# A transformer layer on 8 cores: four PSUM banks in turn for the qkv projection, and one cast moved from VectorE to GpSimd

## The reference

```python
x = x + attn_a(layernorm(x))     # causal, rotary embedding, softmax
x = x + ffn(layernorm(x))
x = x + attn_b(layernorm(x))     # not causal, rotary, q and k normalised
x = x + ffn(layernorm(x))        # same weights as the first ffn

def ffn(x):
    h = bit_linear(x, w1)                      # 1024 -> 4096
    h = silu(depthwise_conv1d(h, conv_w))      # three taps along the tokens
    return bit_linear(h, w2)                   # 4096 -> 1024

def bit_linear(x, w):            # x rounded to integers by a scale per token,
    ...                          # w rounded to -1, 0, 1
```

## Time and profile before

| | us |
|---|---|
| median of the runs before (2 runs: 4828.32 and 4828.6) | 4828.46 |
| the profiled execution, its own time | 4822.62 |
| its span on the slowest core | 4821.1 |
| spans of the 8 cores | 4804.7 to 4821.1 |

### The profile page before, as it was taken

How to read it: one execution, slowest core, us unless ns; L and a number is a source line. 1 busy time by engine, 2 the same in 40 slices (tenths; PEclk the granted TensorE clock), 3 DMA queues, 4 the chain that set the end, 5 groups by cost and what they waited for, 6 DMA issues and landing times.

```text
span 4821.1 us, 43781 instructions; the slowest of 8 cores (4804.7 to 4821.1 us)
## 1 busy us (share of the span) xinstructions
PE 2901.5 (60%) x11610; PEld 993.1 (21%) x11610; DVE 1946.7 (40%) x3077; ACT 1947.7 (40%) x2092; POOL 506.5 (11%) x1034
## 2 busy tenths in 40 slices
PE   2455456656564456757545555777777835658665
PEld 0122111111112222323212221111111212223222
DVE  3323222222225676776533331010110166767763
ACT  0222145555440324224034444777777513242240
POOL 0000022222222001001001110000000110011010
PEclk9777666666676789989877777888878868889898
DMA  6333343322210123323231113000010001223224
GB/s 152 105 97 94 99 92 90 82 75 76 80 38 1 50 70 96 101 70 110 70 64 27 27 27 60 16 16 16 16 26 6 3 1 60 83 72 114 77 90 136
DMA packets 321185, 311.21 MB, mean 65 GB/s; under 512 B 213648, under 2 KB 226224, under 8 KB 320944
## 3 DMA queue, kind: packets, MB, share of 16 engines
q1 hardware_dynamic: 316272, 291.62, 21.4%
q0 software_dynamic: 4672, 16.79, 2.1%
HBM read 270.46 MB, written 50.46 MB: 67 GB/s over the span
## 4 chain that ended last, share of the span: by engine, by line
PE 29%; DVE 23%; ACT 18%; issue 12%; DMA 10%; POOL 4%; SPq 1%; DVEq 1%; ACTq 0%; POOLq 0%
PE pb L587 6%; PE pb L378 6%; PE pb L612 5%; ACT expqb L559 5%; PE squad L546 4%; DMA wq_tmp<-w2T 3%; ACT qkbfb L397 3%; PE squad L1065 3%; PE pb L659 2%; DMA wq_tmp<-w1T 2%; PE pb L908 2%; DVE hqi_B L1098 2%; DVE hqi_DD L1098 2%; DVE hdeq_DD L999 2%; DVE hdeq_B L999 2%
## 5 line engine op out<-in xcount | busy, mean ns | idle before, releaser
L559 ACT ACTIVATE expqb<-squad,kconst 128x1024 bf16<-128x1024 f32 x512 | 566.3, 1113 | 211.0 <-PE pb L587 167.2
L559 ACT ACTIVATE expqa<-squad,kconst 128x1024 bf16<-128x1024 f32 x320 | 351.2, 1112 | 304.8 <-PE pb L587 225.4
L587 PE MATMUL pb<-expqb,vbufb 128*65 128x512 bf16 x1024 | 363.4, 441 | 0.8 <-ACT expqb L559 0.8
L587 PE MATMUL pb<-expqa,vbufa 128*65 128x512 bf16 x640 | 258.8, 495 | 125.3 <-POOL expqa L571 117.5
L378 PE MATMUL pb<-Wqkva,lnTa 128*128 128x512 bf16 x768 | 212.0, 426 | 174.4 <-DVE lnTa L373 174.4
L1065 PE MATMUL squad<-xqfm_B,wbuf_B 128*128 128x512 bf16 x1024 | 246.5, 384 | 112.4 <-DVE hdeq_B L999 107.5
L1065 PE MATMUL squad<-xqfm_DD,wbuf_DD 128*128 128x512 bf16 x1024 | 246.2, 384 | 112.1 <-DVE hdeq_DD L999 109.3
L908 PE MATMUL pb<-w2buf_DD,hsilu_DD 128*128 128x512 bf16 x1024 | 265.7, 392 | 52.1 <-DMA w2buf_DD<-w2qT_d 30.5
L908 PE MATMUL pb<-w2buf_B,hsilu_B 128*128 128x512 bf16 x1024 | 263.2, 387 | 52.7 <-DMA w2buf_B<-w2qT_d 26.7
L546 PE MATMUL squad<-qbufb,kbufb 64*128 64x512 bf16 x1024 | 228.5, 436 | 108.6 <-ACT expqb L559 78.8
L1023 ACT ACTIVATE cvo_B<-hdeq_B,tapb_B,tapw_B 128x512 f32<-128x512 f32 x128 | 104.1, 813 | 433.6 <-POOL hdeq_B L1010 235.5
(11 more groups left out here) (219 smaller groups left out, 4284.4 us busy)
## 6 DMA issues: line engine op xcount, KB each, us to landing
wq_tmp<-w1T SPq DMA_DIRECT2D x64, 512.0 KB, 4.8
wq_tmp<-w2T SPq DMA_DIRECT2D x64, 512.0 KB, 4.0
wbuf_B<-w1qT_d SPq DMA_DIRECT2D x128, 256.0 KB, 2.6
w2buf_B<-w2qT_d SPq DMA_DIRECT2D x128, 256.0 KB, 2.7
wbuf_DD<-w1qT_d SPq DMA_DIRECT2D x128, 256.0 KB, 2.6
w2buf_DD<-w2qT_d SPq DMA_DIRECT2D x128, 256.0 KB, 2.8
x<-x SPq DMA_DIRECT2D x16, 512.0 KB, 28.7
w1qT_d<-wq_bf SPq DMA_DIRECT2D x32, 256.0 KB, 2.9
```

Of the source, the lines that this page charges most:

```text
L559: sb.op("act", lambda e, sqh=sqh, eb=eb: e.activation(out=expq[eb][:, 0:1024], in_=squad[:, sqh * 1024:(sqh + 1) * 1024], func=AF.Exp, sca ...
L587: sb.op("pe", lambda e, i=i, hi=hi, v0=v0, eb=eb, ob=ob, first=first, last=last: e.matmul(pbank[ob + hi][0:65, :], vbuf[i][:, v0:v0 + 65], ...
```

## The change

Two edits. In the first part of both attentions the six groups of a chunk take the banks `pbank[0]` to `pbank[3]` in turn instead of `pbank[0]` and `pbank[1]`; the keys follow. (The added `g=g` in three lambdas has no effect on what is issued.) In the quantising loop of the FFN the cast from int32 to bf16 is issued on POOL instead of DVE; its operands and keys are as before.

```diff
--- before.py
+++ after.py
@@ -373,36 +373,36 @@
         sb.op("dve", lambda e, i=i, tps=tps: e.tensor_copy(out=lnT[i][:], in_=tps),
               reads=[("sq", 0)], writes=[("lnT", i)])
         for g in range(6):
-            pb = pbank[g % 2]
+            pb = pbank[g % 4]
             for dc in range(NDC):
                 sb.op("pe", lambda e, i=i, dc=dc, g=g, pb=pb: e.matmul(
                     pb[:], lnT[i][:, dc * 128:(dc + 1) * 128],
                     Wqkv[dc][:, g * 512:(g + 1) * 512],
                     start=(dc == 0), stop=False),
-                    reads=[("lnT", i), ("Wqkv", dc)], writes=[("pb", g % 2)])
+                    reads=[("lnT", i), ("Wqkv", dc)], writes=[("pb", g % 4)])
             sb.op("pe", lambda e, g=g, pb=pb: e.matmul(
                 pb[:], onesbf[0:1, :], battrow[0:1, g * 512:(g + 1) * 512],
                 start=False, stop=True),
-                reads=[("onesbf",), ("battrow",)], writes=[("pb", g % 2)])
+                reads=[("onesbf",), ("battrow",)], writes=[("pb", g % 4)])
             if g < 4:
                 if causal:
                     dst = qkbf[i][:, g * 512:(g + 1) * 512]
-                    sb.op("act", lambda e, dst=dst, pb=pb: e.activation(
+                    sb.op("act", lambda e, dst=dst, pb=pb, g=g: e.activation(
                         out=dst, in_=pb[:], func=AF.Identity),
-                        reads=[("pb", g % 2)], writes=[("qkbf", i)])
+                        reads=[("pb", g % 4)], writes=[("qkbf", i)])
                 else:
                     dst = qkbf[i][:, g * 512:(g + 1) * 512].rearrange(
                         "p (h b a) -> p h a b", b=2, a=32)
                     src0 = pb[:].rearrange("p (h a b) -> p h a b", a=32, b=2)
-                    sb.op("act", lambda e, dst=dst, src0=src0: e.activation(
+                    sb.op("act", lambda e, dst=dst, src0=src0, g=g: e.activation(
                         out=dst, in_=src0, func=AF.Identity),
-                        reads=[("pb", g % 2)], writes=[("qkbf", i)])
+                        reads=[("pb", g % 4)], writes=[("qkbf", i)])
             else:
                 h0 = (g - 4) * 8
                 vv = vstage[i][:].rearrange("p (h c65) -> p h c65", c65=65)[:, h0:h0 + 8, 0:64]
-                sb.op("act", lambda e, pb=pb, vv=vv: e.activation(
+                sb.op("act", lambda e, pb=pb, vv=vv, g=g: e.activation(
                     out=vv, in_=pb[:].rearrange("p (h q) -> p h q", q=64), func=AF.Identity),
-                    reads=[("pb", g % 2)], writes=[("vstage", i)])
+                    reads=[("pb", g % 4)], writes=[("vstage", i)])
         if pending[0] is not None:
             pending[0]()
         qv = qkbf[i][:].rearrange("p (g2 h i2) -> p g2 h i2", h=2, i2=32)
@@ -1099,7 +1099,7 @@
                 out=hqi[:], in0=hsilu[:, jc * 512:(jc + 1) * 512], in1=squad[:, 0:512],
                 op=ALU.mult),
                 reads=[("hsilu", jc), ("sq", 0)], writes=[("hqi",)])
-            sb.op("dve", lambda e, jc=jc: e.tensor_copy(
+            sb.op("pool", lambda e, jc=jc: e.tensor_copy(
                 out=hqb_all[:, jc * 1024:jc * 1024 + 512], in_=hqi[:]),
                 reads=[("hqi",)], writes=[("hsilu", jc)])
             if jc == 0:
```

## The result

| | before | after |
|---|---|---|
| median of all runs, us | 4832.27 (10 runs) | 4888.02 (11 runs) |
| profiled execution: span of the slowest core | 4821.1 | 4871.7 |

The ratio of after to before is 1.0106, 95% interval 1.0079 to 1.0132: 51 us slower (38 to 64). The prediction was 118 us slower, with a range from 57 to 222 us (4885 to 5050 against 4828). The sign and the place are right; the size is less than half. The loss is clear of no change, but it lies within the 2% to which the prediction gave 34 in 100.

A forecast was written before the change was run, and what follows sets the result against it. No engine bounds the whole kernel; DVE's product and cast pace the quantising loop, ACT the second attention's first part. Banks 0, casts 109 and clock 9 make 118 us over 4828: 4946 us, range 4885 to 5050.

The forecast's parts named there:

- What bounds the loop: Quantising loop of the FFN: 32 DVE steps of 1.32 us, product and cast with gaps, plus a short end.
- The banks are worth nothing: First part of both attentions: four banks instead of two gain 0, bounds 0 and -24.3 us; ACT sets the pace.
- The step as product + handover + X + handover: Quantising loop, one block after the change: 0.686 + 0.21 + X + 0.10 = 0.996 + X us, against 1.32.
- X: Time of one quantising-loop cast on POOL, taken as 0.75 us; 256 casts add 109 us.
- the prediction's own sign: Quantising loop: the forecast is wrong if the cast L1102 on POOL takes under 0.67 or over 1.1 us.
- The handover from DVE to POOL at 0.21: Quantising loop: from the product's end on DVE to the cast's start on POOL, 0.21 us, read from L422.
- The clock, 9 us: Quantising loops' ends and next tiles' starts: a lower TensorE clock adds 9 us, bounds 0 and 17.
- Rival 1: Quantising loop: POOL casts as fast as it writes, 0.53 to 0.67 us; +53 to +88 us; 33 in 100.
- Rival 2: Quantising loop: integer conversion is slow on POOL, 1.1 us or more a cast; 5093 us at 1.29; 8 in 100.
- Rival 4: Quantising loop: DVE and POOL hinder each other, 0.33 us a cast, 84 us more, 5030; 1 in 100.
- The price from the skill: Quantising loop's cast on POOL: 769 ns for 512 elements from a skill page, adding 114 us instead of 109.
- Rival 3: Quantising loop: product and cast overlap, PE's 1.02 us sets the step, 77 us less, 4752; 2 in 100.

The follow-up runs named there:

- experiment 2: The kernel before with only the four banks, the cast staying on VectorE: ratio 0.9979 (0.9955 to 1.0002).
- experiment 7: The full change with hqi in f32, rounding to integers left out: the cast on GpSimd takes 0.609 us.
- experiment 13: The full change with the cast replaced by a GpSimd add of two different f32 tiles, hqi and amac, into bf16: the add takes 1.26 us.
- experiment 8: The full change with the cast replaced by a GpSimd add of hqi (f32) to itself: add 1.04 us, some 160 us slower than before.
- experiment 3: The full change with two hqi buffers and keys instead of one: ratio 0.9970 to the kernel before, 15 us faster than it.
- experiment 14: The full change with the cast on ScalarE instead of GpSimd, still one hqi buffer: ratio 1.0151 to the kernel before, 73 us slower.

## Why the prediction was right and wrong

- *What bounds the loop: right.* 32 steps of DVE set its length before; the round trip sets it after, with every product waiting for POOL's L1102 (105.1 us in 124 waits for the first FFN).
- *The banks are worth nothing: right*, as far as the times can tell (experiment 2) and by the stage's length in the traces, 467.3 and 465.4 us.
- *The step as product + handover + X + handover: right in form.* With the measured terms it gives 0.69 + 0.13 + 0.61 + 0.10 = 1.53, and 54 us for 256 blocks, against 51 measured.
- *X = 0.75: the term that was most out.* It measured 0.609, 0.141 less, or 36 us of the sum. By the prediction's own sign (L1102 under 0.67) the forecast was wrong. The text had the right figure, 0.62, from the copy of two columns and the memsets' 0.86 ns a column, and put it aside for two reasons. One was that the integer might cost something: experiment 7 shows that it doesn't. The other was half of the two-input row L669. That row adds two different tiles, and experiment 13 shows that such a second input costs 0.65 us where the first costs 0.43. The row to halve was L428 in the earlier trace rows, which squares one tile: (1.89 - 0.18) / 1024 / 2 is 0.83 ns a column, and with 0.18 that makes 0.61. The prediction's 1.63 ns a column mixed that row with L571, which reads two different tiles.
- *The handover from DVE to POOL at 0.21: out as well.* It measured 0.13, 0.08 less, or 20 us. I read it from one pair of rows and gave it no bounds, although shows another: L1010 starts 0.13 us behind the L999 that released it (started at 2001.97, 0.68 us long). The 0.21 holds a second semaphore wait, 0.06 us, that L1102 does not have behind VectorE's. The range was built from X alone, and that is why its lower end, +57 us, which needs X = 0.55 with 0.21, lies above the 51 us that came out with X at 0.609.
- *The clock, 9 us: about nothing.* The granted clock in the first loop is 0.95, as in the earlier trace rows, with PE busy 33.54 of 49.60 us (68%), not the 58% that the longer step would have made. The tile behind the third loop starts with eight matmuls in 1.89 us, the upper level, where the earlier trace rows had 3.32. And the earlier trace rows was not the rule: of the six tiles behind a quantising loop on the slowest core, four started in 1.89 us before the change and two at the lower level, and after it all six in 1.89. So the term was priced from an exception. In experiment 8, with a step of 1.97 us, the loop's granted clock is 0.85, so a longer step can lower it; 1.53 us did not.
- 36 + 20 + 9 = 65 of the 67 us by which the forecast missed: the mechanism was right, and three terms of its sum were too large.
- *Rival 1 (POOL casts as fast as it writes) is what happened* as to X: 0.609 lies in its 0.53 to 0.67, and the result in the band of no change that it named. Its 53 to 88 us carried the same 0.21; with 0.13 it reads 33 to 68.
- *Rival 2 (slow conversion) fell* with experiment 7. *Rival 4 (the engines hinder each other) fell* with experiment 3: 0.609 us for the cast, alone or beside the product. The product reads one operand from SBUF and one from PSUM. The Trainium skill, page "SBUF — State Buffer", section "SBUF: two separate sides", has the lock only for DVE instructions with two SBUF inputs or in a two-port mode. The trace of experiment 3 agrees: the loop was spared with overlap too.
- *The price from the skill*, 769 ns for 512 elements (the Trainium skill, page "GPSIMD Engine Reference", section "3.1 Elementwise — side-by-side cycle accounting"), was no better than mine. The same section has a second rate, 1.03 cycles an element for small loop bodies (its k ≤ 2). At the 1.2 GHz that it uses this is 0.86 ns, an estimate, and the measured 0.83 ns a column is near it. The prediction had cited the other of the two.
- *Rival 3's price was wrong.* It took PE for the limit with overlap, 77 us under before. Experiment 3, which built just that, gained 15: the `w2` loads come first. The trace of before had shown it, in the last stretch of the FFN, which takes 40.1 us for the same matmuls.

## What to carry to other kernels

Work moved to an idle engine gains little while one buffer ties the two engines together: the step becomes both durations plus two handovers. It pays only if the moved part and the two handovers together take less than the old engine spent on that part with its gaps (here 0.84 us against 0.63). Give the pair a second buffer first, then look for the wait that takes over (here the weight loads, hidden behind casts until then), and only then count the gain: with two `hqi` buffers and earlier loads the move gained 101 to 117 us, where this change lost 51. When a cost has no row, keep the estimate that is built from rows of the same kind (for an instruction with two inputs, see first whether they are the same tile), and put bounds on every term of the sum, the small handovers too: 0.08 us was 20 us over 256 blocks. Before a handover is taken from a row, count the semaphore waits of that instruction, and see which comes last.

## What the runs showed of the hardware

- A GpSimd cast of 128x512 takes 0.609 us from int32, int16 or f32 alike; 0.396 at 256 columns. VectorE takes 0.427 us from int32 and 0.294 from int16.
- A GpSimd add of a tile to itself takes 1.04 us and of two different tiles 1.26, both 512 columns of f32 into bf16. Beyond the fixed 0.18 us, the same tile twice costs twice one input; a different tile costs more.
- A semaphore wait that follows the one that counts delays the start even if it is long fulfilled: 0.06 us on GpSimd (L669 0.20 us behind VectorE with it, 0.15 without), 0.07 on VectorE (0.17 us behind ACT with it in experiment 14; L413 starts 0.10 behind ACT without it in the earlier trace rows).
- GpSimd casts at full speed while VectorE multiplies an SBUF operand by a PSUM operand.
- One PSUM bank brought TensorE's granted clock in the second attention's first part down to 0.62 (0.79 with two, 0.75 with four), and its median matmul from 379 to 634 ns. The step of a group became 6.5 us, where matmuls at the upper level and the wait for ACT had been worked out to 4.9.
